# Up half of a two-layer network in seven block products: order of loads, of VectorE's and ScalarE's steps, and places of the scatters

## What is computed

```python
ys = cond * 512 ** -0.5
d = rsqrt(ys*ys @ (w*w) + 1e-8)
xf = ((x * ys) @ w) * d                      # 4096 x 512
top1 = argmax(softmax(xf @ gate_w.T))
masked = xf * one_hot(top1)                  # per expert
h = relu(masked @ w1 + b1)                   # 2 experts, 512 -> 2048
routed = (h @ w2 + b2).sum(experts)
shared = relu(xf @ sw1 + sb1) @ sw2 + sb2
out = x + routed + shared
```

## Time and profile before

| | before |
|---|---|
| median of 3 runs | 1463.98 us (1463.56 to 1464.52) |
| the profiled execution's own time | 1463.63 us |
| its span, first to last instruction | 1460.7 us |
| TensorE busy | 1425.5 us, 98% |
| VectorE busy | 847.2 us, 58% |
| ScalarE busy | 501.4 us, 34% |
| GpSimd busy | 314.4 us, 22% |
| up half, first to last matmul | about 102 to 438.5 us |

### The profile page before, as it was taken

How to read it: one execution, slowest core, us unless ns; L and a number is a source line. 1 busy time by engine, 2 the same in 40 slices (tenths; PEclk the granted TensorE clock), 3 DMA queues, 4 the chain that set the end, 5 groups by cost and what they waited for, 6 DMA issues and landing times.

```text
span 1460.7 us, 17708 instructions
## 1 busy us (share of the span) xinstructions
PE 1425.5 (98%) x6262; PEld 1175.8 (80%) x6262; DVE 847.2 (58%) x1362; ACT 501.4 (34%) x776; POOL 314.4 (22%) x354
## 2 busy tenths in 40 slices
PE   9997999999999999999999999999999999999998
PEld 8776778877877888888888888888888888888886
DVE  7895887857777878777864514224245532423235
ACT  4453553535454444444533211111123221111112
POOL 0000000062132110000023240614215151340533
PEclk9999899999999999999999999999999999999999
DMA  6947548494778898977675220312106231120312
GB/s 207 248 159 201 216 177 238 167 260 173 242 263 279 277 298 261 287 256 233 214 214 169 60 50 11 66 20 47 39 14 201 60 62 26 29 57 2 66 22 33
DMA packets 157190, 215.66 MB, mean 148 GB/s; under 512 B 46560, under 2 KB 67552, under 8 KB 157120
## 3 DMA queue, kind: packets, MB, share of 16 engines
q1 hardware_dynamic: 142240, 186.71, 39.9%
q0 software_dynamic: 14880, 28.07, 9.4%
HBM read 131.19 MB, written 85.75 MB: 149 GB/s over the span
## 4 chain that ended last, share of the span: by engine, by line
PE 75%; DVE 2%; issue 1%; DMA 1%; POOL 0%; ACT 0%; SPq 0%; another core or an unknown queue 0%; POOLq 0%; DVEq 0%; ACTq 0%
PE bank L1965 24%; PE bank L1989 23%; PE bank L1930 20%; PE bank L1893 8%; PE bank L1985 0%; DMA hin<-hidden_scratch 0%; DVE xw L1281 0%; DVE vb L1351 0%; DMA hidden_scratch<-vb 0%; POOL out L766 0%; DVE vt L1327 0%; DVE vb L1333 0%; DVE hl L1312 0%; DMA out<-res,tab 0%
## 5 line engine op out<-in xcount | busy, mean ns | idle before, releaser
L1893 PE MATMUL bank<-xw,w_hi 128*128 128x512 f32 x896 | 281.6, 396 | 22.5 <-DVE vb L1351 16.0
L749 POOL DMA_INDIRECT rows_e<-xf_scratch,soft x144 | 145.1, 1007 | 663.5 <-PE bank L1930 265.1
L1694 DVE CAST h_hi<-hf 128x512 fp32r<-128x512 f32 (+1 forms) x128 | 56.9, 445 | 387.3 <-ACT hf L1073 329.5
L1930 PE MATMUL bank<-hl,w_hi 128*128 128x512 f32 x896 | 277.3, 391 | 3.4 <-DVE hl L1312 3.3
L1073 ACT ACTIVATE hf<-bank,b 128x512 f32<-128x512 f32 (+1 forms) x128 | 87.4, 683 | 545.9 <-PE bank L1965 426.2
L1893 PEld LDWEIGHTS bank<-xw,w_hi 128*128 128x128 f32 x896 | 170.1, 191 | 62.6 <-DVE vb L1351 17.5
L1930 PEld LDWEIGHTS bank<-hl,w_hi 128*128 128x128 f32 x896 | 168.8, 189 | 39.6 <-DVE hl L1312 4.7
L1965 PE MATMUL bank<-xe_lo,w_hi 128*128 128x512 f32 (+1 forms) x512 | 197.7, 386 | 0.0
L1965 PE MATMUL bank<-xe_hi,w_hi 128*128 128x512 f32 (+1 forms) x512 | 197.6, 386 | 0.0
L1965 PE MATMUL bank<-xe_hi,w_lo 128*128 128x512 f32 (+1 forms) x512 | 196.0, 386 | 0.0
L1989 PE MATMUL bank<-w_lo,h_hi 128*128 128x512 f32 x496 | 193.0, 389 | 0.0
(11 more groups left out here) (216 smaller groups left out, 1699.3 us busy)
## 6 DMA issues: line engine op xcount, KB each, us to landing
hin<-hidden_scratch SPq DMA_DIRECT2D x112, 512.0 KB
hidden_scratch<-vb SPq DMA_DIRECT2D x80, 512.0 KB
hidden_scratch<-vt SPq DMA_DIRECT2D x32, 512.0 KB
stage<-w_pack SPq DMA_DIRECT2D x64, 256.0 KB
ring<-x_cols SPq DMA_DIRECT2D x32, 256.0 KB, 4.0
xf_scratch<-xo SPq DMA_DIRECT2D x32, 256.0 KB, 3.7
raw<-w_shared SPq DMA_DIRECT2D x32, 256.0 KB, 4.3
rows<-xf_scratch SPq DMA_DIRECT2D x16, 512.0 KB
```

What stands on the lines that cost most here:

```text
L749: pool.indirect_dma_start(rows_e[:, c % JN, :], None, xf_dram, bass.IndirectOffsetOnAxis(tab_rows[:, c:c + 1], 0)).then_inc(rows_gathered, ...
L1694: nc.vector.tensor_copy(h_hi[:, buf, 0:filled_n], hf[:, j % 2, 0:filled_n]).then_inc(hh_ready, 4)
L1893: last = nc.tensor.matmul(up_bank(u, UP_BANK[c])[p][:], w[:, DOWN_W[c], pair, part], xw[:, c, x, k, :], start=(c in FRESH and n == 1), sto ...
L1930: last = nc.tensor.matmul(bank[p][:], w[:, DOWN_W[c], i, part], hl[:, n % HL, h, :], start=(i == 0 and q == 0), stop=(i == PAIRS - 1 and q ...
```

## The change

The projection: the second weight's sums move from tile 16 to 15 and its split from 17 to 16, the third's sums from tile 23 to the start of group 0; the places of the x blocks and of their sums move apart. The order of the x operands becomes 0 to 6.

SP: the four row loads of the next block go to four places (after product 5's store of g = 0, before t4's store of g = 1, after that of g = 1, before t4's of g = 2) in place of all four in g = 1; in groups 1 and 2 the weight load stands ahead of the row load. Weights 8 to 11 are all loaded in group 12, into places of their own. The first three hidden loads move from the start of group 15 to the end of group 14, ahead of t1's, t2's and vb21's stores of that group.

VectorE: `make_t4(u - 1)` moves to the head of the group, ahead of the first job's `raw_sums` and of the x operands 5 and 6. The adds of product 3 go ahead of the second job's `raw_sums`. The flips move from the start of g = 2 to its end; `slots` and `places` to the end of groups 5 and 8. At a block change all three first sums of x stand ahead of the adds.

ScalarE: at a block change `block_hi(s + 1, 1)` stands ahead of the take of product 2; in group 15 the first casts of hidden units stand behind it.

GpSimd: a scatter for every two products-and-pairs in place of one for every 0.875; the table is read from group 14 on, spread, in place of from group 12 on.

```diff
-RAW_AT = (13, 17)
-SUMS_AT = (12, 16, 23)
+RAW_AT = (13, 16)
+SUMS_AT = (12, 15)
 FLIP_AT = (18, 19, 20, 21)
-X_AT = (22, 24, 26, 28, 30)
+X_HI_AT = (21, 24, 26, 27, 29)
+X_LO_AT = (22, 25, 27, 28, 30)
+X_SUM_AT = (23, 24, 26, 29)
...
-TABLE_GROUP = 12
+TABLE_GROUP = 14
...
-X_ORDER = (0, 1, 3, 2, 4, 5, 6)
-X_DONE = tuple(X_ORDER.index(c) + 1 for c in range(STEPS))
...
-RAW_FIRST = {0: (4,), 1: (6,), 12: (8, 9), 13: (10, 11), 14: (12, 13)}
+RAW_FIRST = {0: (4,), 1: (6,), 12: (8, 9, 10, 11), 14: (12, 13)}
 RAW_SECOND = {0: (3,), 1: (5,), 2: (7,)}
+ROWS_BEFORE = {1: 1, 2: 3}
+ROWS_AFTER = {0: 0, 1: 2}
 RAW_LAST = 2 * PAIRS - 2
-RAW_KB = (208, 196, 160, 164)
-RAW_HOME = (0, 0, 0, 0, 0, 0, 0, 0, 0, 1, 0, 1, 0, 1, 2, 3)
+RAW_KB = (208, 184, 188, 192, 196, 160, 164)
+RAW_HOME = (0, 0, 0, 0, 0, 0, 0, 0, 1, 2, 3, 4, 0, 4, 5, 6)
 RAW_USE = tuple(RAW_HOME[:n].count(home) for n, home in enumerate(RAW_HOME))
 
...
                 if n == PAIRS:
+                    sp.wait_ge(xw_lo, STEPS * BLOCKS)
+                if n == PAIRS + 4:
                     sp.wait_ge(ids_out, NT * DMA)
-                if n == PAIRS + 1:
-                    sp.wait_ge(xw_lo, STEPS * BLOCKS)
...
-            def next_rows(s):
+            def next_rows(s, q):
 
                 sp.wait_ge(xw_lo, STEPS * (s + 1))
-                for q in range(QD):
-                    sp.dma_start(rows[q * B32:(q + 1) * B32, :, :], quad_rows(q, s + 1)).then_inc(rows_in, DMA)
+                sp.dma_start(rows[q * B32:(q + 1) * B32, :, :], quad_rows(q, s + 1)).then_inc(rows_in, DMA)
 
             def keep(src, s, g, c):
...
-                if n == 0:
-                    sp.wait_ge(xw_lo, STEPS * BLOCKS)
-                if n == 3:
-                    sp.wait_ge(raw_ready, RAW_LAST)
-                    sp.wait_ge(sums_made, 4 * RAW_LAST)
+                if n < LOADS:
+                    in_place = max(m for m in range(2 * PAIRS) if RAW_KB[RAW_HOME[m]] == 184 + 4 * n)
+                    sp.wait_ge(raw_ready, in_place + 1)
+                    sp.wait_ge(sums_made, 4 * (in_place + 1))
...
-                    if last:
-                        for n in range(LOADS - 1):
-                            hidden_load(n)
                     if u > 0:
                         keep_t3(u - 1)
-                    if g == 1 and s < BLOCKS - 1:
-                        next_rows(s)
                     for n in RAW_SECOND.get(u, ()):
                         raw_load(n)
+                    if g in ROWS_BEFORE and s < BLOCKS - 1:
+                        next_rows(s, ROWS_BEFORE[g])
                     if u > 0:
                         keep_t4(u - 1)
...
+                    if g in ROWS_AFTER and s < BLOCKS - 1:
+                        next_rows(s, ROWS_AFTER[g])
                     for n in RAW_FIRST.get(u, ()):
                         raw_load(n)
+                    if u == GROUPS * BLOCKS - 2:
+                        for n in range(LOADS - 1):
+                            hidden_load(n)
                     if last:
...
-                pool.wait_ge(up_mm, PER_GROUP * SCATTER_GROUP + c * 7 // 8)
+                pool.wait_ge(up_mm, PER_GROUP * SCATTER_GROUP + 2 * c)
...
+                    pool.wait_ge(up_mm, PER_GROUP * TABLE_GROUP + 5 * i)
...
+                        pool.wait_ge(up_mm, PER_GROUP * TABLE_GROUP + 5 * i + q + 1)
...
                 take(vb22, 1, 1, ACT.Identity)
                 for n in jobs[:1]:
                     raw_sums_hi(n)
-                if last:
-                    first_units(0, 2)
+                if more:
+                    block_hi(s + 1, 1)
                 wait(act, t1_out, DMA * u)
                 take(vt1, 2, 0, ACT.Identity)
                 if more:
-                    block_hi(s + 1, 1)
                     block_hi(s + 1, 2)
+                    block_hi(s + 1, 3)
+                if last:
+                    first_units(0, 2)
+                act.wait_ge(up_added, 6 * u + 2)
+                nc.scalar.activation(vb11[u % 2][:], vb11[u % 2][:], ACT.Relu).then_inc(b11_made, 1)
                 for n in jobs[1:]:
                     raw_hi(n)
+                if more:
+                    block_hi(s + 1, 4)
                 if last:
                     first_units(2, 4)
-                act.wait_ge(up_added, 6 * u + 2)
-                nc.scalar.activation(vb11[u % 2][:], vb11[u % 2][:], ACT.Relu).then_inc(b11_made, 1)
-                if more:
-                    block_hi(s + 1, 3)
+                act.wait_ge(up_added, 6 * u + 4)
+                nc.scalar.activation(vb22[:], vb22[:], ACT.Relu).then_inc(b22_made, 1)
                 for n in jobs[1:]:
                     raw_sums_hi(n)
                 if last:
                     first_units(4, 6)
-                act.wait_ge(up_added, 6 * u + 4)
-                nc.scalar.activation(vb22[:], vb22[:], ACT.Relu).then_inc(b22_made, 1)
-                if more:
-                    block_hi(s + 1, 4)
-                if last:
-                    first_units(6, HL)
                 if u == 0:
                     for i in range(RING):
                         act.wait_ge(xf_out[i], DMA * NT // RING)
                 wait(act, t4_out, DMA * u)
                 take(vb21, 6, 1, ACT.Relu)
+                if last:
+                    first_units(6, HL)
...
+                if u > 0:
+                    make_t4(u - 1)
+                for n in jobs[:1]:
+                    if n > 1:
+                        raw_sums(n)
                 if g == 0:
                     for i in range(X_EARLY, STEPS):
                         block_lo(s, i)
-                if g == 2 and s < BLOCKS - 1:
-                    for i in range(FLIPS):
-                        flip(s + 1, i)
                 for n in jobs[:1]:
-                    if n > 2:
-                        raw_sums(n)
                     raw_lo(n)
                     raw_sums_lo(n)
                 if u == CHOOSE_GROUP:
                     choose()
                 if u == RANK_GROUP:
                     count()
-                    slots()
-                if u == PLACE_GROUP:
-                    places()
-                if u > 0:
-                    make_t4(u - 1)
+                if more:
+                    block_lo(s + 1, 0)
+                    x_sum_of(s + 1, 0)
+                    x_sum_of(s + 1, 1)
+                    block_lo(s + 1, 1)
+                    x_sum_of(s + 1, 2)
+                add(vb11[u % 2], 3, 0, 0)
+                if more:
+                    block_lo(s + 1, 2)
+                add(vb11[u % 2], 3, 0, 1)
                 for n in jobs[1:]:
                     raw_sums(n)
-                if more:
-                    block_lo(s + 1, 0)
-                    x_sums(s + 1, 0)
-                    block_lo(s + 1, 1)
-                    x_sums(s + 1, 1)
-                if last:
-                    units_lo(0, 2)
-                add(vb11[u % 2], 3, 0, 0)
-                add(vb11[u % 2], 3, 0, 1)
+                add(vb22, 4, 2, 0)
                 for n in jobs[1:]:
                     raw_lo(n)
-                add(vb22, 4, 2, 0)
-                if more:
-                    block_lo(s + 1, 2)
-                    x_sums(s + 1, 2)
                 add(vb22, 4, 2, 1)
                 if more:
                     block_lo(s + 1, 3)
+                    x_sum_of(s + 1, 3)
+                if last:
+                    units_lo(0, 2)
+                add(vt1, 5, 4, 0)
+                add(vt1, 5, 4, 1)
                 for n in jobs[1:]:
                     raw_sums_lo(n)
-                add(vt1, 5, 4, 0)
-                add(vt1, 5, 4, 1)
                 if more:
                     block_lo(s + 1, 4)
                 if u == 0:
...
                     units_lo(2, 4)
                 make_t1(u)
                 if last:
+                    units_lo(4, 5)
                     raw_sums(RAW_LAST)
                     raw_lo(RAW_LAST)
-                    units_lo(4, 6)
+                    units_lo(5, 6)
                 make_t2(u)
                 if last:
                     raw_sums(RAW_LAST + 1)
                     raw_lo(RAW_LAST + 1)
                     units_lo(6, HL)
                 make_t3(u)
+                if g == 2 and s < BLOCKS - 1:
+                    for i in range(FLIPS):
+                        flip(s + 1, i)
+                if u == RANK_GROUP:
+                    slots()
+                if u == PLACE_GROUP:
+                    places()
```

More of the change, by code:

```diff
@@ L1302, in _ @@
                     raw_sums(SUMS_AT.index(c))
-                if c in X_AT:
-                    block_lo(0, X_AT.index(c))
-                    if X_AT.index(c) < 3:
-                        x_sums(0, X_AT.index(c))
+                if c in X_LO_AT:
+                    block_lo(0, X_LO_AT.index(c))
+                if c in X_SUM_AT:
+                    x_sum_of(0, X_SUM_AT.index(c))
             def units_lo(n0, n1):
@@ L1858, in up_group @@
                     if g == 0:
```

(2 more changed lines are left out.)

26 lines of the change are left out of this document (13 added, 13 removed).

## The result

| | before | after |
|---|---|---|
| median, measured side by side | 1463.77 us | 1481.05 us |
| ratio, with its 95% interval | | 1.0112 (1.009 to 1.0133) |
| the profiled execution's own time | 1463.63 us | 1482.09 us |
| its span | 1460.7 us | 1480.1 us |
| up half, first to last matmul | 102.0 to 438.7 us | 103.0 to 456.4 us |

What follows compares the result with a forecast made beforehand. TensorE, busy 98% of the span, was taken as the bound, so only its waits and slow clock count: up half 39.6 less 28.3, +11.3, projection +3.1, down half -0.5, together +13.9 on 1463.63, giving 1477.5 us (1469 to 1487).

Steps and rivals of the forecast that it cites:

- The step that decides: Groups with a first job: make_t4 at the head holds product 4 until vb21's store lands plus 5.5 us.
- Rival A: Up half: vb21's store lands early enough, by group start (S) + 5.4, so the kernel gets faster, 1454 us; chance 0.15.
- rival D: Hidden loads, table reads and weights collide in group 15 and carry on into the down half: +12, 1490 us; chance 0.05.
- Group 13: Up half: four weights loaded in group 12 delay vb21's store to group start + 10.6; loss 6.8 us against 0.
- Group 15: Up half's end: three hidden loads ahead delay vb21's store by 3.9 us to group start + 15.2; loss 12.0 us.
- Rival C: Group 1: the weight is still late as row loads share the queue, 12.7 us stay; 1484.5 us; chance 0.10.
- Group 3: Block change: flips end at about group start + 7.2 and block_hi(1) delays product 2's take; loss 1.5 us against 1.41.
- Group 4: ScalarE's first take stands behind softmax exponentials, made late by VectorE's end of group 3; loss 3.2 us against 1.52.
- The scatters: Groups 9 to 11: waits fall within scatters, now at half the rate; 2.5 us taken, half of 4.9.
- The projection: The wait for the second weight comes one tile earlier, at tile 20: idle 4.5 us, clock 1.5; +3.1 us.
- The down half's start: Cast, weight 14 and hidden load 3 chain as before, one unit earlier: 0.5 us won.
- The alternative of 1469.5: Whole kernel: only the longest wait pays a slow clock restart, 8 us less than 1477.5.

Runs made afterwards that it cites:

- e1: The changed kernel with make_t4 back behind the first job, all else as changed: 1450.07 us, ratio 0.9959 to the kernel before.
- e2: The kernel before with make_t4 at the head of the group and nothing else: 1483.95 us, ratio 1.0181.
- e4: The changed kernel with weights 8 and 9 loaded in group 12 and 10 and 11 in group 13: 1476.82 us, ratio 1.0137 to the kernel before.
- e3: The changed kernel with the three hidden loads back at the start of group 15: 1473.14 us, ratio 1.0116 to the kernel before.
- e7: The changed kernel with make_t4 behind the first job, hidden loads at group 15's start, projection's second weight at tiles 16 and 17: 1448.18 us, ratio 0.9905.
- e6: The changed kernel, unchanged, profiled a second time beside the kernel before: 1480.85 us, ratio 1.0132.
- e8: e7 with the take of product 2 ahead of block_hi(s + 1, 1): 1446.19 us, ratio 0.9894 to the kernel before.
- e11: e10 with products 0 to 2 taken ahead of the next block's high halves, product 3's adds behind its first sum: 1447.06 us, ratio 0.9928.
- e9: e7 with the scatters' old pace: 1447.29 us, ratio 0.9929 to the kernel before.
- e10: e7 with another order of ScalarE's and VectorE's work at the down half's start: 1445.65 us, ratio 0.9924 to the kernel before.
- e12: The kernel before with only the weight load moved ahead of the four row loads in SP's queue: 1449.14 us, ratio 0.9947.

## Why the prediction was right

**The step that decides** held within 0.2 us. The working put the restart of product 4 at landing + 5.5, so the wait at landing - (S + 5.4). The landings of the table, 8.7, 9.3, 12.6, 6.6 and 17.1, give 3.3, 3.9, 7.2, 1.2 and 11.7; the waits are 3.46, 3.96, 7.26, 1.24 and 11.76. e1 and e2 show the cause from both sides, once taken out, once put in alone. Rival A, by which the store lands in time, is out with the landings, and of rival D, by which the loss carries on into the down half, there are 1.7 us.

**Sizes of landings** were short where the queue is full. Group 2: 9.3, where its forecast idle of 2.8 meant 8.2. Group 13: 12.6 against 10.6. The working took 2 us for two more weights; e4 gives 3.0, and its own landing with two is S + 9.6, not the 8.8 of the earlier trace rows. Group 15: 17.1 against 15.2. The working divided 1.5 MB by 397 GB/s, 3.9 us; e3 measures 5.9, two thirds of that rate. The windows view after, the stretch while these loads and stores are under way (after the clock: share of the DMA engines, GB/s):

```profile
430.00:435.00 5.00, 3.52 (x16) 2.59 (x14) 0.00 (x0) 0.00 (x0) 0.00 (x0) 1.00 1.16 218
435.00:440.00 5.00, 0.00 (x0) 0.00 (x0) 0.28 (x1) 0.00 (x0) 1.24 (x1) 0.76 0.92 343
440.00:445.00 5.00, 0.00 (x0) 0.00 (x0) 4.03 (x7) 3.29 (x5) 1.13 (x1) 0.50 0.45 110
```

At a full share (1.16) the engines move 218 GB/s in the first five microseconds, as the row loads did in the earlier trace rows (214), and 343 at a share of 0.92 in the next, nowhere the 397 that the working took. That rate came from a stretch with another mix of transfers; which transfer sets it was not tried.

**Group 1** was right, 5.3 against 5.5, and group 14, 1.5 against 1.8. Rival C, that the weight is late anyway, is out: group 1's wait at product 6 is gone.

**Group 3** was the worst term, 6.3 against 1.5, 4.8 us. The working took the flips' end at S + 7.2; it is S + 9.4 in after and in e7. `make_t2` starts at S + 2.3 in both, while in before it is at S + 0.7, and these 1.6 us were not in the sum. The rows of VectorE say where they come from. The change puts `raw_sums_lo` of the second job behind product 5's adds; before, it stood ahead of them (171.36, the adds at 172.23). Now it stands right ahead of `make_t1` with 0.65 us of wait and 0.96 of work; before, then after:

```profile
171.36 0.95 DVE L1268 TENSOR_TENSOR w_lo<-sums,w_hi 128x768 fp32r<-128x768 f32 x1
```
```profile
172.16 0.96 DVE L1273 TENSOR_TENSOR w_lo<-sums,w_hi 128x768 fp32r<-128x768 f32 x1 [0.65 <-ACT w_hi L882]
```

The later end of the flips is 2.2 us; with the slow stretch of 2.3 us that follows a wait of this length, which a loss of 1.5 had not held, it makes up nearly all of the difference. No run puts `raw_sums_lo` back alone, and e6, the same kernel, had a wait of 2.41 there with `make_t2` at S + 0.8, so the size of this term is not firm. Neither of the two exchanges tried, e8 and e11, wins time by it.

**Group 4** was counted twice, 3.2 against 0. TensorE came to group 4 late by group 3's own wait, so VectorE's lateness had already been paid. This is read from the trace and not shown by a run of its own: where group 3 waits about 4 us, group 4 has from 0 (after, e9, e10) to 0.82 us (e7), and where group 3's wait is gone, in e11, whose order is another, 5.54. A wait that is forecast must be carried into the start of the next group.

**The scatters** were given 2.5 us and cost none. (Of the two waits that this term rests on, shows only that of 2.03 us.) After has no wait in groups 8 to 10, but e9 none either with the old pace, so the pace alone is not the cause. Before shows such a wait in both its profiles, e2 and e12 none in their one; the cause stays open.

**The projection** gave 1.6 us in place of 3.1. The wait moved to one tile earlier as said; VectorE stands 6.63 us for the weight and TensorE 3.81:

```profile
66.26 0.42 DVE L1237 TENSOR_TENSOR sums<-raw 128x256 f32<-128x256 f32 x1 [6.63 <-DMA raw<-w_shared]
```
```profile
68.59 0.50 PE L1829 MATMUL bank<-w_hi,x_hi 128*128 128x512 f32 x1 [3.81 <-DVE x_lo L1142]
```

The weight itself landed 1.3 us before the 67.51 of the earlier trace rows. Over all profiles the stretch holds 5.6 us in the five with the sums at tile 15 (3.4 to 7.2) and 3.8 in the nine with tile 16 (1.3 to 6.3), so these 1.8 us are less than the scatter within either.

**The down half's start** lost 1.7 where 0.5 was to be won. e7 and e10 show how VectorE's and ScalarE's order makes waits there; what set them in after itself was not tried.

**The sum.** Up half 47.0 less 30.7, +16.3; projection +1.6; down half's start +1.7; together 19.6, and the spans differ by 19.4. The forecast had +11.3, +3.1 and -0.5. Groups 2, 3, 13 and 15 were 13.0 us too small and the down half's start 2.2, group 4, the scatters and the projection 7.2 too large, and before's own loss in the up half, which is taken off, was put at 28.3 and is 30.7. So the spans differ by 5.5 us more than the forecast: the direction and the mechanism were right, but that 1477.5 came within 3.6 us of the median (2.5 of that of the three) is in part luck, of terms that cancel and of the level of the executions.

**The clock.** 41.9 of after's 60.2 us are idle, the other 18.3 nearly all slow clock. Each of the five waits of the up half from 3.46 us up has its slow stretch, as in the windows view after, behind group 1's wait of 3.46:

```profile
136.00:138.00 2.00, 1.48 (x5) 1.20 (x6) 2.00 (x3) 1.04 (x2) 0.00 (x0) 0.81 0.69 163
138.00:140.00 2.00, 2.00 (x7) 1.54 (x6) 0.40 (x2) 1.06 (x1) 0.00 (x0) 0.50 0.99 256
140.00:142.00 2.00, 2.00 (x9) 1.66 (x8) 1.93 (x6) 1.05 (x1) 0.00 (x0) 0.84 1.05 314
```

That is the rule which the forecast weighed (the Trainium skill, TensorE: Matmul & The Clock Gate, HAM oscillation — how this bites in real kernels): a slow restart at every stop. The trace agrees for the long stops: 18.3 us in after for five long waits in the up half, one in the projection and one in the down half. Behind the three short ones of the up half (1.08, 1.08 and 1.24 us) the granted clock stays at 1.00, so not every stop pays. The alternative of 1469.5, with one restart only, would have missed by more than 10 us.

## What to carry to other kernels

Before a step goes to the head of an in-order queue, follow what it waits for and everything behind it on that engine and the next: here one instruction of 1.2 us that waits for a store held up three engines and cost 22 to 32 us. Loads wanted late should not be issued ahead of stores that something waits for soon; put the transfer whose landing ends the nearest wait first, and ask which store is then last. When a wait is moved, add it to the next group's start before costing that group.

## What was not expected of the hardware

**What stands ahead of a load set most of its time, but not all.** A 512 KB weight took 10.1 us from issue (133.31) to landing (143.45) behind four row loads, 3.85 us ahead of four (e12), 4.4 and 6.1 us ahead of one row load and the stores after it (after, groups 1 and 2: issued at 135.27 and 160.18, landed at 139.66 and 166.30). With more behind it, in e12, it was not slower. The Trainium skill, DMA: Bandwidth & Descriptors, Queues, rings and completion order, says that on each DMA engine descriptors are consumed in ring order; the 10.1 against 3.85 agree, while the spread from 3.85 to 6.1 with the weight in front is not in it, and no run here takes it apart.

**Issuing early had a price.** The same page, Rules for kernel authors, says to issue a DMA early and wait for it late. Here that cost 5.9 us (e3), since the stores behind the loads were what the next step waited for.

**The granted clock fell behind some waits of 2.0 to 2.6 us and not behind others.** Two waits of 2.29 us at the down half's start, e10's and e11's, in windows view:

```profile
430.00:432.00 2.00, 1.42 (x6) 1.05 (x6) 1.90 (x3) 1.93 (x4) 1.12 (x1) 1.00 0.07 29
432.00:434.00 2.00, 0.59 (x3) 0.31 (x3) 2.00 (x3) 0.18 (x1) 0.00 (x0) 1.00 0.57 110
```
```profile
432.00:434.00 2.00, 1.12 (x3) 0.94 (x4) 1.96 (x3) 2.00 (x4) 1.12 (x1) 0.75 0.09 37
434.00:436.00 2.00, 1.79 (x6) 0.87 (x4) 1.94 (x3) 0.38 (x1) 0.00 (x0) 0.50 0.80 149
```

e10 keeps 1.00 (2.4 GHz), e11 falls to 0.50 (1.2 GHz). Both had a shorter wait just before, of 1.38 and 1.29 us. What tells the two apart is open; in e11's two windows it cost 1.5 us.
